# Expert blocks two batches earlier in the second layer, and the scatter ahead of them at twice the rate

## The chip, the cores and the metric

The kernel runs on one core of a Trainium2 chip. The metric is the device time of one execution in microseconds (us); the median of three runs before the change is 831.46 us (830.25 to 831.56). The engines are PE (TensorE, matrix products; PEld is its loading of weights), DVE (VectorE), ACT (ScalarE), POOL (GpSimd) and SP (SyncE, which issues most DMAs). Each works through its own queue of instructions in order and waits for the others on semaphores.

## The reference

The input x is 8 batches of 512 tokens with 128 features. Two layers follow one another, each of the form

```
xn = layernorm(x)
x  = x + attention(xn) * silu(ffn(xn))
```

Layer 0 has a causal attention with one head and a feed-forward part with a dense branch and 6 experts, of which two are taken per token. Layer 1, which the change touches, is

```
q = (xn @ Mq).reshape(B, 8, 512, 64)      # 8 heads of 64
k = (xn @ Mk).reshape(B, 8, 512, 64)
v = (xn @ Mv).reshape(B, 8, 512, 16)
s = softmax(q k^T / 8 over keys) v        # with the reference's own order of axes
e = argmax(xn @ Wg + bg)                  # one of 8 experts per token
y = relu(xn @ W1[e] + b1[e]) @ W2[e] + b2[e]
x = x + s * silu(y)
```

Everything is in float32.

## The kernel before

Layer 0 runs first, up to about 400 us of the span; the change does not touch it. It leaves the normalized rows of layer 1 in xn_all (32 tiles of 128 tokens, NT = 32), their transpose in xn2T, and a one-hot row of the chosen expert for each token.

Layer 1 has two kinds of work.

Attention goes batch by batch (B = 8), and within a batch over 16 steps, numbered through as k = 0 to 127 (IT = 16 in a batch). In step k PE makes two score tiles of 128 x 512 (score(k), L1334, called S(k) below) into a pair of PSUM banks; DVE takes their maximum (L1579); ACT takes the exp into pb and the row sums (L1446); DVE inverts the sums into rz (L1555); POOL scales the values by them into vs (L1255); and PE multiplies vs with pb (value(k), L1319, called V(k) below). PE runs value three steps behind score (LAG = 3): its queue holds S(k), V(k-3), then a "mixed" piece if the table MIXED has one for this step, then S(k+1). Mixed pieces are the projections of the next batch's q and k (L1293, one for every odd step), of its v (L1301, step 6), and the turning of finished heads (L1307, steps 4 and 12). DVE stores them (L1531, L1525, L1540) ahead of its rz of k-2 and its maximum of k. The first score of a batch waits until the last projection for it is stored. The bodies of the batches are written out, not looped.

The experts work on tokens sorted by expert. DVE computes from the one-hot rows a slot in DRAM for each token. Then POOL scatters the 32 tiles of xn_all to x_sorted by indirect DMA (L1243), one tile per DMA. SP waits until all 32 have landed (t_sc) and then loads blocks of 128 sorted tokens; there are NB = 39 blocks, each of one expert. A block is loaded, transposed by PE (L1374), multiplied with W1 (L1378), transposed again in four parts (L1386), multiplied with W2 (L1394), and stored to y_sorted by SP. The stages of following blocks overlap (function blocks). The 39 blocks run as one stretch on SP, PE, ACT and DVE, with no attention between them. Their buffers lie in xn_all, which the scatters have read by then.

Function layer1 sets the order for every engine: attention batches 0 to BEFORE-1, then all blocks, then attention batches BEFORE to 7. POOL has no blocks; it goes on with the next batch when rz arrives.

POOL's body counts a batch in 32 steps n (ST = 32, two for each k). At each n, in this order: scatters, if the batch lies before the blocks; at even n the vs of k = n/2; and, in batches 4 to 7 (kind SUMS), the gathers of y_sorted by indirect DMA (L1269, four in a row of n from 3 and from 19, each set for one quarter of the sum of two batches) and three products and sums over them (L1226, L1230, L1233). How many scatters have been issued after step `now` (counted through the batches from 0) is `(now + 1) * 3 // 8`, up to 32. In batches 4 to 7 ACT also takes a tanh of the gathered rows, and SP stores the output at the end of each sum.

Of the kernel before, what the change touches and what calls it, by code (L numbers as in the profile page):

```python
# [19 lines left out]
def recurrent_d2_kernel(nc, x, W, b, ln_g, ln_b, aw1, ab1, aw2, ab2, gate_w, gate_b, ew1, eb1, ew2, eb2,  # L20
# [9 lines left out]
    NT = B * TT  # L30
# [18 lines left out]
    with ExitStack() as ctx:  # L49
# [1114 lines left out]


        PLAIN, SUMS = range(2)
        BEFORE = 4
        GATHER_AT = (3, SH + 3)
        SUM_AT = (5, GEN + 5)
        LOAD = -2  # L1170
# [19 lines left out]
        def layer1(eng, body, make=None, enter=None, leave=None):  # L1190
            for bt in range(BEFORE):
                body(bt, PLAIN, False)
            if make:
                eng.wait_ge(t_ex, 1)
                if enter:
                    enter()
                blocks(eng, make)
                if leave:
                    leave()
            for bt in range(BEFORE, B):  # L1200
                body(bt, SUMS if bt >= B // 2 else PLAIN, bt == B - 1)

        @blk.gpsimd
        def _(pool):
# [16 lines left out]
            def sum_up(k, part):  # L1221
                rows = bass.ds(k * TT, TT)
                if part == 0:
                    pool.wait_ge(g_th, k * 2 + 2)
                    pool.wait_ge(g_st, k * 16 + 16)
                    pool.tensor_tensor(ob[:, :, :], th3[:, :, :], yg[:, :, :], ALU.mult).then_inc(g_c, 1)  # L1226
                elif part == 1:
                    pool.wait_ge(mb_free, turn_use(k * 2 + 1) + 1)
                    pool.wait_ge(g_c, k * 2 + 1)
                    pool.tensor_tensor(ob[:, :, :], ob[:, :, :], s1[:, rows, :], ALU.mult).then_inc(g_c, 1)  # L1230
                else:
                    pool.wait_ge(g_c, k * 2 + 2)
                    pool.tensor_tensor(ob[:, :, :], ob[:, :, :], x_all[:, rows, :], ALU.add).then_inc(g_o, 1)  # L1233

            def body(bt, kind, last):
                for n in range(ST):
                    if isinstance(bt, int) and bt < BEFORE:
                        if bt == 0 and n == 0:
                            pool.wait_ge(t_slot, 1)
                            pool.wait_ge(t_z, 1 + 16)  # L1240
                        now = bt * ST + n
                        for g in range(min(now * 3 // 8, NT), min((now + 1) * 3 // 8, NT)):
                            pool.indirect_dma_start(  # L1243
                                out=x_sorted, out_offset=bass.IndirectOffsetOnAxis(ap=slot[:, g:g + 1], axis=0),
                                in_=xn_all[:, g, :], in_offset=None).then_inc(t_sc, 16)
                    if kind == SUMS and n in (2, ST // 2 + 2):
                        pool.wait_ge(g_sl, (bt - 4) * 2 + n // (ST // 2) + 1)
                    if n % 2 == 0:
                        k = bt * IT + n // 2
                        s = k % SLOTS  # L1250
                        if n == 0:
                            pool.wait_ge(mb_free, values_in(bt))
                        pool.wait_ge(n_rz, k + 1)
                        pool.wait_ge(n_av, k + 1)
                        pool.tensor_tensor(vs[s][:, :, :],  # L1255
                                           vt[bt % 2][:, n // 2 % TT, :, :].rearrange("p j d -> p (j d)")
                                           .unsqueeze(1).broadcast_to([P, 2, D]),
                                           rz[:, 2 * s:2 * s + 2].unsqueeze(2).broadcast_to([P, 2, D]),
                                           ALU.mult).then_inc(n_vs, 1)
                    if kind == SUMS and n in (0, ST // 2):  # L1260
                        k = (bt - 4) * 2 + n // (ST // 2)
                        if n == 0:
                            for par in range(2):
                                pool.wait_ge(m_st[par], 16 * ((NB + 1 - par) // 2) + 16)
                        pool.wait_ge(g_o, k + 1)
                        pool.tensor_copy(slot_b[:, :], slot[:, bass.ds(k * TT, TT)]).then_inc(g_sl, 1)
                    t = n % SH - GATHER_AT[0]
                    if kind == SUMS and 0 <= t < TT:
                        pool.indirect_dma_start(  # L1269
                            out=yg[:, t, :], out_offset=None, in_=y_sorted,  # L1270
                            in_offset=bass.IndirectOffsetOnAxis(ap=slot_b[:, t:t + 1], axis=0)).then_inc(g_y, 16)

                    if kind == SUMS and 0 <= n % SH - 2 * SUM_AT[0] - 1 < 3 and not (last and n > SH):
                        sum_up((bt - 4) * 2 + n // SH, n % SH - 2 * SUM_AT[0] - 1)

            layer1(pool, body)
            for part in range(3):
                sum_up(B - 1, part)

        @blk.tensor  # L1280
        def _(pe):
# [117 lines left out]
            def enter():  # L1399
                pe.wait_ge(mb_free, pairs_in(BEFORE))  # L1400
                pe.wait_ge(n_e, 2 * BEFORE * IT + 4)

# [263 lines left out]
```

## Time and profile before

| what | value |
|---|---|
| median of the runs | 831.46 us (830.25 to 831.56) |
| profiled execution, its own time | 831.46 us |
| its span | 829.7 us |
| PE busy | 746.8 us (90%) |
| DVE busy | 582.6 us (70%) |
| ACT busy | 396.6 us (48%) |
| POOL busy | 238.7 us (29%) |
| mean granted clock of TensorE | 0.975 |

A profile is one execution. Spans are counted from its first instruction. "Busy" of an engine is the time in which it executes an instruction; the rest is waiting or issuing. Matmuls are pipelined and their ends are modelled. The granted clock is a share of full speed: 1.00 is 2.4 GHz, 0.50 is 1.2 GHz. In the timeline each row gives the start, the duration, the engine, the line, the operation, what it writes and reads, how many instructions are merged into the row, and in square brackets how long the engine was idle before it and what ended that. "issue" there means that it waited for nothing that the profile shows.

The stages of the span: layer 0 up to 399 us; sorting and the first projections to 417; attention batches 0 to 3 from 417.28 to 563; the blocks from 563.76 to 671.38; attention batches 4 to 7 with the sums from 671.38 to the end.

### The profile page before, as it was taken

The page shows a single profiled execution, that of the slowest core. Times are in us where ns is not written, and L with a number is a line of the kernel's source. Part 1 is how long each engine was busy: PE and PEld are TensorE (multiplying, and loading weights), DVE is VectorE, ACT ScalarE, POOL GpSimd, SP SyncE. Part 2 cuts the span into 40 slices and gives each one's busy share as a digit, 9 for nine tenths or more (in the row PEclk, how much of TensorE's full clock was granted, in tenths as well). Part 3 has the DMA queues.
Part 4 walks back from the last instruction along what each step waited for, and adds up shares of the span by engine and source line. Part 5 has one row for each costly group of instructions (what it writes and reads, how often), then busy time and mean ns, then how long its engine had stood idle before and what let it go on. Part 6 is the DMA issues. An engine that isn't in the chain of part 4 may idle for free. (4 is left out here: it accounts for less than half of the span.)

```text
span 829.7 us, 19914 instructions
## 1 busy us (share of the span) xinstructions
PE 746.8 (90%) x6611; PEld 497.9 (60%) x6612; DVE 582.6 (70%) x1486; ACT 396.6 (48%) x1000; POOL 238.7 (29%) x364
## 2 busy tenths in 40 slices
PE   5989899999999999992789999998999999999983
PEld 3666677888788788882334444444666754444331
DVE  5888864678778778786587878883333368778772
ACT  2332314444344344340056666664444557677782
POOL 7355200000000000000036565320000037676773
PEclk9999999999999999997799999999999999999996
DMA  8600000000000000000500000001111101111110
GB/s 262 209 0 0 1 1 1 1 2 0 0 0 0 0 0 0 0 0 0 150 14 25 23 23 23 11 3 29 51 47 50 48 25 30 30 27 27 40 33 19
DMA packets 34272, 25.04 MB, mean 30 GB/s; under 512 B 3303, under 2 KB 30626, under 8 KB 34210
## 3 DMA queue, kind: packets, MB, share of 16 engines
q1 hardware_dynamic: 31256, 19.48, 8.0%
q0 software_dynamic: 2048, 4.20, 1.8%
q8 instruction: 37, 0.61, 0.3%
q10 hardware_dynamic: 906, 0.55, 0.2%
q14 instruction: 25, 0.20, 0.1%
HBM read 14.91 MB, written 9.31 MB: 29 GB/s over the span
## 5 line engine op out<-in xcount | busy, mean ns | idle before, releaser
L1446 ACT ACTIVATE pb<-bank,nmx 128x512 f32<-128x512 f32 x256 | 173.2, 682 | 70.5 <-DVE nmx L1579 67.7
L1579 DVE TENSOR_REDUCE nmx<-bank 128x2 f32<-128x1024 f32 x128 | 156.4, 1223 | 30.7 <-PE bank L1334 29.2
L1334 PE MATMUL bank<-qk 64*128 64x512 f32 x512 | 144.2, 640 | 10.2 <-DVE qk L1531 5.3
L853 ACT ACTIVATE hid<-bank,cols 128x512 f32<-128x512 f32 x128 | 87.8, 687 | 123.6 <-PE bank L766 123.5
L1255 POOL TENSOR_TENSOR vs<-vt,rz 128x256 f32<-128x256 f32 x128 | 78.4, 613 | 231.0 <-DVE rz L1555 216.8
L1319 PEld LDWEIGHTS bank<-pb,vs 128*32 128x32 f32 x2048 | 48.6, 110 | 101.3 <-issue 72.0
L782 PEld LDWEIGHTS bank<-w_e,hid 128*128 128x128 f32 x768 | 98.1, 191 | 8.2 <-DVE acc L1000 1.7
L782 PE MATMUL bank<-w_e,hid 128*128 128x128 f32 x768 | 100.1, 275 | 0.0
L1319 PE MATMUL bank<-pb,vs 128*32 128x128 f32 x2048 | 83.3, 281 | 5.3 <-POOL vs L1255 5.3
L728 POOL TENSOR_TENSOR r<-ve,half_neg 128x4 f32<-128x4 f32 x8 | 8.1, 1011 | 274.0 <-DVE ve L927 274.0
L1462 ACT ACTIVATE xn_all<-bank,cols 128x128 f32<-128x128 f32 x156 | 44.5, 367 | 51.7 <-PE bank L1386 51.7
L1334 PEld LDWEIGHTS bank<-qk 64*128 64x128 f32 x512 | 38.8, 184 | 47.8 <-ACT pb L1446 25.4
L766 PE MATMUL bank<-xb_hi,w_u_hi 128*128 128x512 f32 x128 | 60.0, 469 | 3.3 <-DVE xb_lo L958 3.3
L1587 DVE COPY xn_all<-bank 128x512 f32<-128x512 f32 x39 | 27.0, 692 | 50.0 <-PE bank L1378 50.0
L1000 DVE SCALAR_TENSOR_TENSOR acc<-bank,wf,acc 128x128 f32<-128x128 f32 x160 | 44.9, 343 | 22.2 <-PE bank L782 20.9
L1531 DVE COPY qk<-bank 128x512 f32<-128x512 f32 x64 | 43.8, 689 | 13.5 <-PE bank L1293 12.5
L1446 ACT ACTIVATION_READ_ACCUMULATOR pb<-bank,nmx 128x1 f32 x256 | 50.5, 197 | 0.0
L766 PE MATMUL bank<-xb_hi,w_u_lo 128*128 128x512 f32 x128 | 50.4, 394 | 0.0
L766 PE MATMUL bank<-xb_lo,w_u_hi 128*128 128x512 f32 x128 | 50.3, 393 | 0.0
L1394 PEld LDWEIGHTS bank<-w,xn_all 128*128 128x128 f32 x312 | 37.9, 191 | 11.9 <-issue 11.7
L1293 PE MATMUL bank<-xn2T,mq 128*32 128x256 f32 x512 | 40.1, 385 | 3.6 <-DVE qk L1531 2.2
L1394 PE MATMUL bank<-w,xn_all 128*128 x312 | 41.6, 276 | 0.4 <-issue 0.4
(225 smaller groups left out, 1235.7 us busy)
## 6 DMA issues: line engine op xcount, KB each, us to landing
x_sorted<-zero SPq DMA_DIRECT2D x1, 2496.0 KB, 12.4
xn_all<-x_sorted SPq DMA_DIRECT2D x39, 64.0 KB, 1.8
y_sorted<-xn_all SPq DMA_DIRECT2D x39, 64.0 KB, 1.6
x_all<-in_L_attn_x_dram SPq DMA_DIRECT2D x8, 256.0 KB, 5.9
w<-in_L_ffn_W_dram SPq DMA_DIRECT2D x1, 2048.0 KB
out_dram<-xn_all SPq DMA_DIRECT2D x8, 256.0 KB
w_u<-in_L_ffn_ew_dram SPq DMA_DIRECT2D x1, 768.0 KB
w_e<-in_L_ffn_ew_dram SPq DMA_DIRECT2D x1, 768.0 KB
```

The source lines that it names most:

```text
L766: mm = pe.matmul(psum[n % NU][:, :], w[:, n * P:(n + 1) * P], x_[:, :], start=(i == 0), stop=(i == 2))
L782: mm = pe.matmul(dst[:, t * P:(t + 1) * P], hid[n % NU][:, t * P:(t + 1) * P], w, start=(first and t == 0), stop=last, skip_group_check=True)
L853: act.activation(hid[n % NU][:, :], psum[n % NU][:, :], ACT.Gelu, bias=col((ROW_AB1 if n < AC else ROW_EB1 - AC) + n), scale=1.0).then_inc ...
L1000: ins = dve.scalar_tensor_tensor(acc[:, t, :], y, wf[:, t, e:e + 1], acc[:, t, :], ALU.mult, ALU.add)
L1255: pool.tensor_tensor(vs[s][:, :, :], vt[bt % 2][:, n // 2 % TT, :, :].rearrange("p j d -> p (j d)") .unsqueeze(1).broadcast_to([P, 2, D]), ...
L1319: mm = pe.matmul(bank[c * 2 * VD:(c + 1) * 2 * VD, at:at + P], vs[k % SLOTS][:, ab, c * 2 * VD:(c + 1) * 2 * VD], pb[k % SLOTS * 2 + ab][: ...
L1334: mm = pe.matmul(psum[score_banks(k) + ab], qk[bt % 2][half, 1, h, 2 * m:2 * m + 2, :].rearrange("p a k -> p (a k)"), qk[bt % 2][half, 0, ...
L1394: mm = pe.matmul(psum[(5, 6)[par]][:, 0:D], hT[par][:, c * P:(c + 1) * P], w_2[:, bass.ds(e * HC + c, 1), :].rearrange("p a d -> p (a d)") ...
L1446: act.activation(pb[s + ab][:, :], psum[score_banks(k) + ab], ACT.Exp, bias=nmx[:, s + ab:s + ab + 1], scale=1.0, accum_out=zz[:, s + ab:s ...
L1462: ins = act.activation(hT[par][:, c * P:(c + 1) * P], psum[(2, 4)[par]][:, c * P:(c + 1) * P], ACT.Relu, bias=cols[:, bass.ds(e * HC + (RO ...
L1531: dve.tensor_copy(qk[bt % 2][:, :, :, g, :], mixed_bank(u)[:, :].rearrange("p (s h k) -> p s h k", s=2, h=HH)).then_inc(mb_free, 1)
L1579: dve.tensor_reduce(nmx[:, s:s + 2], banks[:, score_banks(k):score_banks(k) + 2, :], AX.X, ALU.max, negate=True).then_inc(n_mx, 1)
```

## The change

The number of attention batches ahead of the blocks goes from 4 to 2, and the scatters are issued at 3/4 per step n in place of 3/8, so that all 32 fall into the two batches.

```diff
         PLAIN, SUMS = range(2)
-        BEFORE = 4
+        BEFORE = 2
         GATHER_AT = (3, SH + 3)
...
                         now = bt * ST + n
-                        for g in range(min(now * 3 // 8, NT), min((now + 1) * 3 // 8, NT)):
+                        for g in range(min(now * 3 // 4, NT), min((now + 1) * 3 // 4, NT)):
                             pool.indirect_dma_start(
                                 out=x_sorted, out_offset=bass.IndirectOffsetOnAxis(ap=slot[:, g:g + 1], axis=0),
                                 in_=xn_all[:, g, :], in_offset=None).then_inc(t_sc, 16)
```

The sums stay in batches 4 to 7. Before, the scatters fell into steps 2 to 85 of 128; now into steps 1 to 42 of 64, at every n that is not a multiple of four.

## Rows read from the trace of the kernel before

**Rows 1.** The page, busy time: us, share of the span, instructions.
```profile
PE 746.8 (90%) x6611; PEld 497.9 (60%) x6612; DVE 582.6 (70%) x1486; ACT 396.6 (48%) x1000; POOL 238.7 (29%) x364
```
**Rows 2.** Windows, batches 1 to 3: stretch, length, busy per engine, clock, DMA, GB/s.
```profile
453.07:489.75 36.68, 35.58 (x464) 16.43 (x465) 30.02 (x52) 24.35 (x67) 21.86 (x28) 1.00 0.07 23
489.75:526.42 36.67, 35.58 (x464) 16.43 (x465) 30.02 (x52) 24.34 (x67) 19.84 (x26) 1.00 0.08 23
526.42:563.10 36.68, 35.58 (x464) 16.41 (x464) 30.05 (x51) 24.35 (x67) 9.80 (x16) 1.00 0.01 2
```
**Rows 3.** Timeline of PE, the first score of batch 1.
```profile
453.07 1.13 PE L1334 MATMUL bank<-qk 64*128 64x512 f32 x4 [0.91 <-DVE qk L1531]
```
**Rows 4.** Timeline of POOL: vs(0), first scatter, three rows around vs(3), vs(16).
```profile
423.14 0.61 POOL L1255 TENSOR_TENSOR vs<-vt,rz 128x256 f32<-128x256 f32 x1 [22.52 <-DVE rz L1555]
423.97 1.25 POOL L1243 DMA_INDIRECT x_sorted<-xn_all,slot  x1 [0.22 <-issue]
...
427.08 1.01 POOL L1243 DMA_INDIRECT x_sorted<-xn_all,slot  x1 [0.16 <-issue]
428.12 0.62 POOL L1255 TENSOR_TENSOR vs<-vt,rz 128x256 f32<-128x256 f32 x1
428.90 1.01 POOL L1243 DMA_INDIRECT x_sorted<-xn_all,slot  x1 [0.17 <-issue]
...
458.71 0.60 POOL L1255 TENSOR_TENSOR vs<-vt,rz 128x256 f32<-128x256 f32 x1 [1.31 <-DVE qk L1531]
```
**Rows 5.** Windows: the blocks, batches 4 and 5, the entry of the blocks.
```profile
563.76:671.38 107.62, 99.79 (x586) 70.87 (x586) 38.41 (x79) 51.30 (x195) 0.00 (x0) 0.98 0.16 46
671.38:708.05 36.67, 35.58 (x464) 16.41 (x465) 29.89 (x52) 24.53 (x65) 22.33 (x30) 1.00 0.10 26
708.05:745.19 37.14, 35.65 (x464) 16.42 (x465) 30.10 (x52) 26.57 (x71) 25.81 (x33) 1.00 0.11 30
...
565.00:570.00 5.00, 4.11 (x10) 1.75 (x10) 1.03 (x2) 1.54 (x6) 0.00 (x0) 0.68 0.09 28
```
**Rows 6.** Timelines of POOL, SP, PE: last scatter, first load, first product of the blocks.
```profile
518.35 1.01 POOL L1243 DMA_INDIRECT x_sorted<-xn_all,slot  x1 [0.15 <-issue]
...
521.51 0.81 SPq L1625 DMA_DIRECT2D xn_all<-x_sorted  x2
...
563.76 0.30 PE L1374 MATMUL bank<-ident,xn_all 128*128 128x128 f32 x1 [1.57 <-ACT pb L1446]
```
**Rows 7.** Timeline of PE, a value product of batch 5.
```profile
732.30 0.65 PE L1319 MATMUL bank<-pb,vs 128*32 128x128 f32 x16 [0.40 <-POOL vs L1255]
```
**Rows 8.** Timeline of POOL, two gathers in a row and the vs behind them.
```profile
681.86 1.00 POOL L1269 DMA_INDIRECT xn_all<-y_sorted,slot_b  x1
683.16 0.95 POOL L1269 DMA_INDIRECT xn_all<-y_sorted,slot_b  x1 [0.30 <-issue]
684.12 0.63 POOL L1255 TENSOR_TENSOR vs<-vt,rz 128x256 f32<-128x256 f32 x1
```
**Rows 9.** Timeline of PE: V(0), V(1), V(19), V(20).
```profile
423.81 0.64 PE L1319 MATMUL bank<-pb,vs 128*32 128x128 f32 x16
...
426.31 0.65 PE L1319 MATMUL bank<-pb,vs 128*32 128x128 f32 x16
...
467.11 0.64 PE L1319 MATMUL bank<-pb,vs 128*32 128x128 f32 x16
...
469.83 0.64 PE L1319 MATMUL bank<-pb,vs 128*32 128x128 f32 x16
```
**Rows 10.** Groups of POOL from 420 to 520 us: count, busy us, mean ns, idle before.
```profile
L1243 POOL DMA_INDIRECT x_sorted<-xn_all,slot x32 | 32.5, 1015 | 5.2 <-issue 5.2
```
**Rows 11.** Windows of 5 us, for the granted clock.
```profile
795.00:800.00 5.00, 3.80 (x46) 1.48 (x48) 3.55 (x5) 4.08 (x12) 3.00 (x5) 1.00 0.07 16
800.00:805.00 5.00, 3.73 (x56) 1.61 (x53) 3.27 (x7) 4.32 (x14) 4.69 (x7) 1.00 0.18 52
380.00:385.00 5.00, 0.00 (x0) 0.00 (x0) 4.39 (x9) 0.30 (x1) 0.00 (x0) 0.75 0.00 0
```

## The prediction

> **What bounds the kernel now.** I began with the busy times and the 40 slices, then cut the second layer into its stages with the windows view, and then read the timelines of POOL and PE side by side. The busy times give PE 90% of the span [rows 1], but the share is an average over two layers; what decides is the stage that the change touches. The windows by batch [rows 2] say more. In the second layer an attention batch takes 36.68 us with scatters on POOL (the batch at 453.07), 36.67 with scatters in about three quarters of it (at 489.75) and 36.68 with none (at 526.42). PE is busy 35.58 us in each. So PE paces these batches, and the scatters cost nothing today: taking them out of a batch gains nothing. The clock is 1.00 in all three, the 2.4 GHz level. PE's one long idle piece in a batch is the 0.91 us at its boundary [rows 3], where the first score waits for DVE to store a projection that PE itself has just made. It is a round trip behind PE's own work, so it moves with PE and absorbs no delay.
>
> The batch pace gives the budget. A batch is 16 steps k: per k a pair of scores S(k), then the value product V(k-3), sometimes a projection. 36.68 / 16 = 2.29 us for one k, 4.59 us for two. Per k POOL makes one vs of 0.61 us; an indirect DMA occupies it for 1.01 us [rows 4]. POOL's steps n are two to a k: n even holds a vs, and any n may hold a scatter, issued ahead of that n's vs.
>
> **The change, part by part.** It has two edits: BEFORE 4 to 2 moves the 39 expert blocks from behind batch 3 to behind batch 1, and the rate of the scatters goes from 3/8 to 3/4 per step n. Nothing is added or removed: the number of scatters (32), gathers, blocks and attention steps stays.
>
> *The move.* All queues carry the blocks together. Their 107.62 us [rows 5] stay, since their loads, products and stores are the same and POOL has nothing in them. At the entry PE waits for the last exp (1.57 us idle, [rows 6]) and a stretch of 5 us shows a mean clock of 0.68 [rows 5]; the batch ahead of the entry has the same order of work, so I leave both as they are. At the exit the next batch is now plain instead of one with gathers. The batch with gathers behind the blocks took 36.67 us [rows 5], as short as a plain one, so nothing is gained there. Of the later batches with gathers, the one at 708.05 took 37.14: 0.40 us of it is one value product that waited for vs [rows 7]. That hangs on when gathers land; I cost it at 0, with 0.5 us either way. On SP, the move brings the wait for all scatters nearer to the first load. Today the last scatter is issued at 518.35 and the first load starts at 521.51, 42 us ahead of the blocks at 563.76 [rows 6]. With the change the 32nd scatter falls in step n = 42, that is k = 21 of 32, and ten steps k, some 23 us, remain before the entry. The load, its landing and this wait stay hidden. If that cover were gone, each microsecond would be paid in full.
>
> *The rate.* Today's pattern has 3 scatters in 8 steps n (four k): POOL needs 4 x 0.61 + 3 x 1.01 plus gaps, under 6.5 us of 9.17. The new pattern has 3 scatters in 4 steps (two k): vs, scatter, scatter, vs, scatter. Starts in the timeline price it [rows 4, 8]:
> - vs to the DMA behind it: 0.78 us (428.12 to 428.90).
> - DMA to the vs behind it, POOL not waiting: 1.04 us (427.08 to 428.12).
> - DMA to DMA: the scatters of before never stand back to back; the gathers do: 681.86 to 683.16, 1.30 us, and 0.96 from the second to the vs behind it (683.16 to 684.12). For the second scatter of a pair I take 1.00 to its vs, the middle of 0.96 and 1.04.
>
> Two k then need 0.78 + 1.30 + 1.00 + 0.78 + 1.04 = 4.90 us of POOL against PE's 4.59. POOL becomes the bound for as long as scatters last. A late vs(k-3) holds V(k-3) at the head of PE's queue, and behind it the projection of this k and S(k+1), so DVE's maximum and ACT's exp of k+1 start late as well; both have slack (DVE is busy 30.02, ACT 24.35 us of a batch of 36.68), PE has none. What absorbs it first is the lead of vs over its value product. That lead is small at the start: vs(0) begins at 423.14 and V(0) at 423.81; V(1) starts at 426.31, so vs(1), which POOL then did right behind the first scatter, was in time; with two scatters ahead of it it is not [rows 4, 9]. At vs(19) the lead has been used up too. I walked POOL step by step from vs(0) to vs(21), letting each PE delay shift all later rz (rz comes from DVE, whose work follows PE's). Each rz is there before POOL reaches its vs (vs(16), which waited for DVE before, began at 458.71 [rows 4]; shifted by the 2.8 us that PE is late by then that is 461.5, and POOL gets there at 462.6), so POOL is never idle in the walk and the delay is plain POOL time.
>
> The last vs that PE must wait for is vs(19), in step n = 38. Before it POOL starts 19 earlier vs and 29 scatters (steps 1 to 38 less the nine multiples of four), 10 of them followed by another scatter, 10 being seconds of a pair, 9 single. So from the start of vs(0): 19 x 0.78 = 14.82; 10 x 1.30 = 13.00; 10 x 1.00 + 9 x 1.04 = 19.36; 0.24 more for the first scatter, which takes 1.25 instead of 1.01 [rows 4]; 0.61 for vs(19); and 0.06 to PE (vs ends at 423.75, V(0) starts at 423.81). Sum 48.09, and 423.14 + 48.09 = 471.23 us. Before, V(19) started at 467.11 [rows 9]. The delay is 4.12 us. vs(20) and vs(21) end ahead of their products as shifted (V(20) lies 2.72 us after V(19) [rows 9]; POOL gets from vs(19) to vs(20) in 0.78 + 1.04), so it grows no further. After that POOL has slack, but PE is the bound and full, so nothing is caught up: blocks and all later batches shift by 4.1 us.
>
> Bounds of the pair's cost: without any gap between two DMAs (1.04 and then 0.96) the sum is 10 x 0.30 less, a delay of 1.1 us; if every first DMA of a pair costs as the one at 423.97 (1.54), and the second 1.04, it is 2.8 more, 6.9 us. The value taken is that of the only back-to-back rows there are. A gain is excluded here: POOL is not the bound of any batch that loses its scatters.
>
> All 32 scatters of before but the first took 1.01 us on POOL (mean 1015 ns), with DVE busy 30.02 of 36.68 us [rows 2, 10]: nothing on DVE held them up. The Trainium skill, page "SBUF — State Buffer", section "SBUF: two separate sides", states the opposite case: a DVE operation in a two-port mode, an fp32 copy within SBUF above all, locks GpSimd out, and descriptors of a DMA issued there cannot be written meanwhile. By that rule the new price per scatter would rise with every such copy. The trace does not bear it out here; it is the third rival.
>
> The profiled execution took 831.46 us, of which 829.7 is span, and it equals the median of the three runs. So the forecast is 831.46 + 4.12 = 835.6 us.
>
> **The rivals.**
> 1. *The scatters stay hidden; not slower.* The place is POOL's queue between 423 and 476. It decides in the cost of two k on POOL: if that is under 4.59 us, the leads hold and nothing moves. For it: the lower bound comes to 0.78 + 1.04 + 0.96 + 0.78 + 1.04 = 4.60, just at the edge. Against: the gathers' 0.30 us gap between the two DMAs [rows 8]. Time 831.5. If, beside that, the clock did not dip at the entry, the 5 us at 0.68 there would shrink to 3.4 and give back 1.6 us: 829.9, and with the 0.4 of [rows 7] 829.5, just faster than the noise.
> 2. *The clock falls under the waits.* PE would wait about 0.2 us per k. The mean granted clock is 0.75 in the 5 us at 380 in which PE did nothing, and 0.68 at the entry, after the idle time there [rows 5, 11]. But from 795 to 805 PE was busy only 3.80 and 3.73 us of 5 and the clock stayed at 1.00 [rows 11]; here PE would be busy some 90% (35.58 of 36.68 + 2.8). Should it fall once, 5 us at the lower level (1.2 GHz) do the work of 2.5: 838.1, more if repeated.
> 3. *Scatters get dearer when denser*, by the 0.24 us that the first one shows: 29 x 0.24 = 7.0 more, 842.6. Against it are the 31 equal durations, and vs, which stayed at 0.60 to 0.63 us beside DVE. The lock that the Trainium skill's page "SBUF — State Buffer" states is a reason why it could be so.
> 4. *The entry waits for scatters or their landing.* 23 us of cover against 3.2 from the last issue to the load [rows 6]: a delay of more than 20 us of POOL would be needed. It would start at 836 and go up.
>
> **How the numbers follow.** Forecast (POOL bound, delay 2 to 6 us) 0.78; rival 1 0.14 (of which 0.04 is faster than noise); rival 2 0.03; rival 3 0.04; rival 4 0.01. Range: the bounds 832.6 (delay 1.1) to 838.4 (delay 6.9), with the 0.5 us of gather landings within; what lies outside is most of rival 1 and rival 3, under 2 in 10. A change within 0.2% (1.66 us) can't be told from none in this kernel: same is 829.8 to 833.1. That takes rival 1 without its faster part and a low end of the forecast, 0.14; faster 0.04; slower 0.82.
>
> **What would show it.** Right: in the changed profile 31 scatters still at about 1.01 us, pairs 1.30 apart; POOL without a wait for rz from 423 to 475; the value products of k = 1, 2, 3, 7, 8, 9, 11 and so on idle before them with POOL's vs as the releaser; the first batch some 2.8 us and the second 1.3 us longer than before; batches from the third on at 36.7 us; blocks at 107.6 us, starting near 494.5. Wrong: both batches at 36.7 (rival 1), a granted clock under 1.00 between 425 and 475 (rival 2), scatters of over 1.1 us (rival 3), or PE idle for a load at the first block (rival 4).

## The result, and the profile after

The changed kernel takes 838.95 us (median of 4 runs, 837.84 to 839.87); the kernel before, on the same chip, takes 831.48 us. The ratio is 1.0096, with a 95% interval of 1.0079 to 1.0114: 7.5 us slower. The forecast of 835.6 us had the sign and named the cause of most of it, but it is 3.4 us short, and 0.6 us outside its range. In two further comparisons, each on a chip of its own, the same kernel came out 1.0072 [1.0058, 1.0085] and 1.0063 [1.0048, 1.0077], 6.0 and 5.2 us slower.

The profiled execution of the changed kernel took 837.39 us (span 835.7), 5.9 us over the profiled one of before and less than any of the four timed runs, so some 1.5 us of the first comparison (838.95 against 837.39) lies in no trace. This execution itself lies inside the forecast's range; the median does not.

The page, busy time; it answers to [rows 1]. No engine does more work; the time is waiting and a lower clock.
```profile
PE 747.9 (89%) x6611; PEld 498.2 (60%) x6612; DVE 582.7 (70%) x1486; ACT 396.7 (47%) x1000; POOL 238.5 (29%) x364
```
Windows of the kernel after, with the columns of [rows 2]: batch 0, batch 1, the blocks, batch 2 (the first behind the blocks), and the batch that answers to the one of 37.14 us in [rows 5].
```profile
418.20:458.32 40.12, 34.06 (x413) 14.94 (x413) 29.47 (x51) 24.51 (x66) 29.41 (x35) 1.00 0.11 35
458.32:495.73 37.41, 37.16 (x464) 16.98 (x464) 29.22 (x50) 23.11 (x63) 21.11 (x28) 0.95 0.08 26
497.24:603.67 106.43, 98.39 (x586) 70.23 (x586) 38.42 (x79) 51.36 (x195) 0.00 (x0) 1.00 0.16 47
603.67:640.34 36.67, 35.58 (x465) 16.43 (x465) 30.12 (x53) 23.96 (x65) 9.80 (x16) 1.00 0.02 4
713.68:750.95 37.27, 35.72 (x464) 16.41 (x465) 30.12 (x52) 26.49 (x71) 25.73 (x33) 1.00 0.11 30
```
Batch 0 took 35.79 us before (first score at 417.28, first score of batch 1 at 453.07 [rows 3]); it takes 40.12 now, 4.33 more. The last batch ahead of the blocks, up to their first product, took 563.76 - 526.42 = 37.34 us [rows 2, 6]; it takes 497.24 - 458.32 = 38.92 now, 1.58 more, with a mean clock of 0.95 in the row that ends at 495.73. Behind the blocks a batch takes 36.67 us as before, and the blocks are 1.19 us shorter, since here the clock stayed at 1.00 through them (0.98 in [rows 5]). The first score came 0.92 us later, in code that the change does not touch. 4.33 + 1.58 - 1.19 + 0.92 is 5.64 of the 5.9 us; the rest is in the later batches (37.27 against 37.14 in the one above).

Timeline of POOL after, the same steps as in [rows 4]: each pair of scatters is as priced.
```profile
424.06 0.61 POOL L1255 TENSOR_TENSOR vs<-vt,rz 128x256 f32<-128x256 f32 x1 [22.36 <-DVE rz L1555]
424.89 1.25 POOL L1243 DMA_INDIRECT x_sorted<-xn_all,slot  x1 [0.22 <-issue]
...
428.21 1.01 POOL L1243 DMA_INDIRECT x_sorted<-xn_all,slot  x1 [0.17 <-issue]
429.25 0.62 POOL L1255 TENSOR_TENSOR vs<-vt,rz 128x256 f32<-128x256 f32 x1
430.04 1.01 POOL L1243 DMA_INDIRECT x_sorted<-xn_all,slot  x1 [0.17 <-issue]
431.35 0.96 POOL L1243 DMA_INDIRECT x_sorted<-xn_all,slot  x1 [0.30 <-issue]
432.33 0.62 POOL L1255 TENSOR_TENSOR vs<-vt,rz 128x256 f32<-128x256 f32 x1
```
430.04 to 431.35 is 1.31 us, 431.35 to the vs 0.98, and two k take 4.91 us (427.42 to 432.33). Over all 32 the scatter costs no more than before [rows 10], here the group of POOL from 420 to 480 us:
```profile
L1243 POOL DMA_INDIRECT x_sorted<-xn_all,slot x32 | 31.9, 998 | 6.9 <-issue 6.6 <-PE bank L1319 0.3
```
Timeline of PE after: two value products that wait for vs, then the boundary of batch 1, which answers to [rows 3], and what follows it.
```profile
428.10 0.65 PE L1319 MATMUL bank<-pb,vs 128*32 128x128 f32 x16 [0.80 <-POOL vs L1255]
...
433.01 0.64 PE L1319 MATMUL bank<-pb,vs 128*32 128x128 f32 x16 [0.52 <-POOL vs L1255]
...
458.32 1.13 PE L1334 MATMUL bank<-qk 64*128 64x512 f32 x4 [2.34 <-DVE qk L1531]
459.38 0.69 PE L1319 MATMUL bank<-pb,vs 128*32 128x128 f32 x16
459.99 2.08 PE L1334 MATMUL bank<-qk 64*128 64x512 f32 x4
462.00 1.08 PE L1319 MATMUL bank<-pb,vs 128*32 128x128 f32 x16
```
The boundary takes 2.34 us instead of 0.91, and the second score pair behind it 2.08 instead of 1.13. The windows show why: TensorE's clock is at its lower level, 1.2 GHz (0.50), from about 460 to 463.
```profile
460.00:462.00 2.00, 2.00 (x8) 0.50 (x4) 0.78 (x2) 1.26 (x4) 1.67 (x3) 0.50 0.10 33
462.00:464.00 2.00, 2.00 (x34) 1.23 (x32) 1.22 (x1) 0.82 (x4) 1.42 (x2) 0.69 0.10 33
```
So there are three things to explain: POOL's queue, which was forecast, and the longer boundary and the dip behind it, which were not.

### The profile page after: what moved, and what is told of

Its sections match the earlier page's. It is cut to its first block and busy times, and to the rows that moved or that the text cites. A ratio compares the mean times of both kernels' runs of the same rounds, so it can differ in the third digit from the quotient of the medians.

```text
span 835.7 us, 19914 instructions
## 1 busy us (share of the span) xinstructions
PE 747.9 (89%) x6611; PEld 498.2 (60%) x6612; DVE 582.7 (70%) x1486; ACT 396.7 (47%) x1000; POOL 238.5 (29%) x364
```

## The experiments

A common measure runs through them: the delay of a score against before, both counted from the kernel's own first score, so that layer 0 drops out. Before, S(15) starts 32.32 us behind the first score, S(16), the first of batch 1, 35.79, S(18) 39.92, and S(31), the last of batch 1, 69.00. I call what is added to the last one the loss of batches 0 and 1; the queue forecast is 4.12. Kernels in one group ran on one chip; "before" is the median there.

**First group (before 830.62 us): the change again, its half without the move, the move at a lower rate, and the scatters replaced by plain work.**

again, the change itself:

> The changed kernel itself, once more, for its profile. Theory A (POOL's queue alone): the loss is POOL's time per two k, the first batch has some 2.8 us of it, and every profile shows the same. Theory B (POOL's queue, and then PE's own stream): a projection's end is signalled about 1 to 1.5 us late once or twice while scatters are dense, and a dip of the clock follows; these differ from profile to profile, so the first score of batch 1 (0.91 us of idle before it in the kernel before, 2.34 in the changed one) may have another value this time. Time 838 to 840 by both.

836.6 us, ratio 1.0072 [1.0058, 1.0085]. In this profile (836.36 us) the boundary and what follows are as before, and S(31) is 4.22 us late. Timeline of PE, the boundary and a value product behind it:
```profile
456.20 1.13 PE L1334 MATMUL bank<-qk 64*128 64x512 f32 x4 [0.91 <-DVE qk L1531]
...
461.77 0.65 PE L1319 MATMUL bank<-pb,vs 128*32 128x128 f32 x16 [0.31 <-POOL vs L1255]
```
The kernel after and this one are the same program; their traces differ from the third projection on.

rate_only, shown against the kernel before:
```diff
-   range(min(now * 3 // 8, NT), min((now + 1) * 3 // 8, NT))    # BEFORE stays 4
+   range(min(now * 3 // 4, NT), min((now + 1) * 3 // 4, NT))
```


> BEFORE stays 4, only the rate of the scatters is 3/4. If the rate alone makes the loss: 836 to 839.5, with batches 0 and 1 as in the changed kernel and 2 and 3 at 36.7 us. If the move of the blocks has a part of its own: at least 2 us less than the changed kernel. If the clock's dip behind the scatters is what costs: the time differs from the changed kernel by one or two dips, 1 to 3 us, in either direction.

835.5 us, 1.0059 [1.0046, 1.0073], S(31) 4.22 us late: the rate alone costs what the queue forecast says, with the blocks where they were.

move_916: BEFORE = 2, rate 9/16.

> BEFORE is 2 as in the change, the rate of the scatters is 9/16: POOL then needs about 15.9 us for 16 steps n against PE's 18.3, and the last scatter is issued in step 56 of 64. Theory A and B: no wait for vs, 830.5 to 832.5, the move alone costs nothing. If the move has a cost of its own (entry, exit, late landing of the scatters): over 834.

832.99 us, 1.0024 [1.0015, 1.0033]. The loss of batches 0 and 1 is 0.14 us. What it costs lies at the entry of the blocks: the last scatter comes 14 steps n later, PE waits 1.90 us and for a load instead of 1.57 for exp, and the clock is at the lower level for some 6.8 us. Timeline of PE, the first product of the blocks:
```profile
491.92 0.30 PE L1374 MATMUL bank<-ident,xn_all 128*128 128x128 f32 x1 [1.90 <-DMA xn_all<-x_sorted]
```

busy: the change, with each scatter replaced by an addition on POOL of nearly the same duration. No scatter is issued, so the experts read zeros; SP waits for 32 counts of t_sc instead of 16 x 32, and an addition waits for the one two before it. The code is shortened at the dots.
```diff
-   pool.indirect_dma_start(out=x_sorted, ..., in_=xn_all[:, g, :]).then_inc(t_sc, 16)
+   row_x = x_all[:, 0:4, :]... [:, 0:496]
+   if g > 1: pool.wait_ge(t_sc, g - 1)
+   pool.tensor_tensor(scr[g % 2][:, :], row_x, row_x, ALU.add).then_inc(t_sc, 1)
```


> The changed kernel with each scatter replaced by an addition on POOL of about the same time in its queue (496 columns, some 1.25 us between the starts around it), so that x_sorted holds only zeros and no scatter DMA runs. Theory A: the time is POOL's, so the delay at the end of the scatters is as in the changed kernel, 836 to 839. Theory B: only the queue part of 2.8 to 4.1 us stays, no projection is signalled late and the clock does not dip behind batch 0: 834 to 836. If instead the traffic of the scatters makes all of it: 831 to 832.

828.88 us, 0.9977 [0.9968, 0.9986]: no loss (0.01 us by S(31)). I had missed the calibration: an addition takes 1.01 us like a scatter, but additions have no issue gap, so two k take 4.05 us. Timeline of POOL (line 1247 is the addition, 1257 the vs):
```profile
437.13 0.61 POOL L1257 TENSOR_TENSOR vs<-vt,rz 128x256 f32<-128x256 f32 x1 [0.34 <-DVE rz L1557]
...
441.18 0.61 POOL L1257 TENSOR_TENSOR vs<-vt,rz 128x256 f32<-128x256 f32 x1
```
It doesn't tell DMA from queue, but it shows that at 4.05 us for two k, under PE's 4.59, nothing is lost, and POOL waits for rz. That it is below before as a whole has its cause at the very end: POOL's closing DRAIN takes 4.01 us in busy and 6.6 us in every kernel with scatters. It is the last thing in the span, so times of kernels with and without scatters differ by 2.6 us for that alone, and the delays by S(31) are what can be compared.

**Second group (before 831.8 us): busy at the right size, and other rates.**

busy640: busy with 640 columns (x_all[:, 0:5, :]).

> The changed kernel with each scatter replaced by an addition of 640 columns on POOL, long enough that two k need about 0.57 + 1.25 + 1.25 + 0.57 + 1.25 = 4.9 us of POOL, as the scatters did (the 496 columns took only 4.05 us for two k, under PE's 4.59, and no value product waited). x_sorted holds zeros, no scatter DMA runs. Theory A (the loss is time in POOL's queue, whatever fills it): the value products wait for vs again, first score of batch 2 some 4.2 us late as with scatters, time about 4 us over that of the 496 columns. Theory B (it is the DMAs' traffic): about as the 496 columns, within 1 us.

832.07 us, 1.0002 [0.9993, 1.0011]. Timeline of POOL, two k:
```profile
437.24 0.61 POOL L1257 TENSOR_TENSOR vs<-vt,rz 128x256 f32<-128x256 f32 x1
437.81 2.46 POOL L1247 TENSOR_TENSOR scr<-x_all 128x640 f32<-128x640 f32 x2
440.23 0.61 POOL L1257 TENSOR_TENSOR vs<-vt,rz 128x256 f32<-128x256 f32 x1
440.80 1.25 POOL L1247 TENSOR_TENSOR scr<-x_all 128x640 f32<-128x640 f32 x1
442.01 0.61 POOL L1257 TENSOR_TENSOR vs<-vt,rz 128x256 f32<-128x256 f32 x1
```
Two k take 4.77 us. The prediction's sum with these starts is 19 x 0.57 + 10 x 2.42 + 9 x 1.21 + 0.61 + 0.06 = 46.59 us from vs(0) to V(19), against 43.97 before [rows 4, 9]: 2.62. The loss measured is 2.66. No scatter is on POOL here, so this loss is POOL's time and needs no transfers. As a whole the kernel equals before mainly because of the DRAIN, here in the views by line of before and of busy640:
```profile
L49 POOLq DRAIN  x1: 6625/6625/6625, 822.8 to 822.8; - x1
...
L49 POOLq DRAIN  x1: 4010/4010/4010, 826.1 to 826.1; - x1
```
Against busy, which has the same DRAIN but ran on another chip, it is 3.2 us slower.

move_58: BEFORE = 2, rate 5/8.

> BEFORE 2, scatters at 5/8 per step n: POOL needs about 17.2 us for 16 steps against PE's 18.3, and the last scatter goes out in step 51, some 13 us ahead of the blocks. Against 9/16 (2.4 us slower than before, last scatter in step 56, first block waits for its load) it tells whether the late landing is what the move alone costs: then 830.5 to 832. If the cost is the clock's dip at the entry of the blocks, which was 6.8 us long in the profiles with BEFORE 2 and 3.4 with BEFORE 4: again 832 to 833.5, with the long dip.

835.1 us, 1.0036 [1.0022, 1.005], loss 2.81 us by S(31), although POOL needs only 17.2 of 18.3 us in eight k. The need fits on average, but a pair of scatters falls on the start, where vs leads by least. Timeline of PE, V(2):
```profile
429.39 0.64 PE L1319 MATMUL bank<-pb,vs 128*32 128x128 f32 x16 [1.02 <-POOL vs L1255]
```

b3_half: BEFORE = 3, rate 1/2.

> BEFORE 3, scatters at 1/2 per step n (step 63 of 96 for the last): two k need 2 x (0.78 + 1.04) = 3.64 us of POOL. No wait for vs is expected. Within 0.7 us of the kernel before if the place of the blocks costs nothing; 1 to 2.5 us over it if moving them from behind batch 3 costs in itself.

832.03 us, 1.0000 [0.999, 1.0011], loss 0. The blocks can move by one batch for nothing when the rate keeps to single scatters.

before_again: the kernel before, as a candidate.

> The kernel before itself, for a profile from the same chip as these three. Same time within 0.2%. Its stages are what the others are compared with: batches of 36.67 us, blocks and entry 111.75 from the last score of batch 3 to the first of batch 4, of which the dip of the clock at the entry is a part that may differ from profile to profile.

832.21 us, 1.0001 [0.9991, 1.0011]: the comparison is good to 0.1%.

**Third group (before 831.47 us): the change twice more, and vs ahead of the scatters of a step.**

> The changed kernel a third time. POOL's queue alone: the first score of the blocks' entry some 4.2 us late against the kernel before (counted from the first score of batch 0). In the first profile of the changed kernel a projection was signalled 1.5 us late at the boundary of batches 0 and 1 and a dip of the clock followed (1.5 us more); the second profile had neither. If that is the common case on some chips, it stands here again and the time is 838 to 840; if it was rare, it is absent and the time is 836 to 838.

> One more profile of the changed kernel, for the same question: is a score of batch 1 late by more than POOL's queue explains, and how long is the clock's dip at the entry of the blocks (3.4 or 6.8 us).

again2: 836.71 us, 1.0063 [1.0048, 1.0077]; again3: 838.29 us, one run. Both profiles have the boundary of 2.31 us and the dip, S(31) 5.92 and 5.91 us late; again3 has a second dip at the entry of the blocks, at 499.1.

vs_first_34 and vs_first_58 (rates 3/4 and 5/8, BEFORE 2): the loop over scatters stands behind the vs of the step instead of ahead of it.
```diff
-   for g in range(...): pool.indirect_dma_start(...)      # scatters of step n
    if n % 2 == 0: ... vs of k = n/2 ...
+   for g in range(...): pool.indirect_dma_start(...)
```


> The changed kernel with the order in a step n turned round: vs first, then the scatter of the same n. The number of DMAs ahead of vs(19) falls by one, the rate stays. Rate theory (POOL needs 4.90 us for two k, PE 4.59): the loss is nearly the same, from the same sums 3.5 us instead of 4.1 at the end of the scatters. Burst theory (the scatter just ahead of a vs is what hurts, not the average): 2 us or less.

> The same turn at 5/8 per step, BEFORE 2. With the scatter first, 5/8 lost 2.8 us in batches 0 and 1 although POOL's average need (17.2 us for 16 steps) lies under PE's 18.3. Burst theory: with vs ahead the loss falls to 1.5 us or less, time 831.5 to 834. If the average were misjudged and POOL is the bound at 5/8 too, the loss stays at 2.5 us or more.

vs_first_34: 836.67 us, 1.0062 [1.0048, 1.0076], loss 5.25 us, more than the 4.22 of again and the 3.5 expected: my expectation was wrong. Behind a vs the order at 3/4 puts the pair ahead of an even k, and V(16) then waits 1.04 us for ACT's oT, which PE did not do before; the fourth group shows why. vs_first_58: 833.15 us, 1.0024 [1.0012, 1.0035], loss 1.78 against 2.81 in move_58, better, but above the 1.5 that I had allowed. Where the average fits, the order helps; at 3/4 it gained nothing.

**Fourth group (before 831.69 us): where the late boundary comes from.** Projections reach DVE late in some profiles. Timelines of DVE, its copies of the last three projections of batch 0, in the kernel after:
```profile
447.63 0.69 DVE L1531 COPY qk<-bank 128x512 f32<-128x512 f32 x1 [1.81 <-PE bank L1293]
452.56 0.69 DVE L1531 COPY qk<-bank 128x512 f32<-128x512 f32 x1 [0.50 <-PE bank L1293]
457.48 0.69 DVE L1531 COPY qk<-bank 128x512 f32<-128x512 f32 x1 [1.78 <-PE bank L1293]
```
and in again:
```profile
445.55 0.69 DVE L1531 COPY qk<-bank 128x512 f32<-128x512 f32 x1 [0.43 <-PE bank L1293]
450.89 0.68 DVE L1531 COPY qk<-bank 128x512 f32<-128x512 f32 x1
455.36 0.69 DVE L1531 COPY qk<-bank 128x512 f32<-128x512 f32 x1 [0.42 <-PE bank L1293]
```
In the first the copies stand 4.9 us apart, which is POOL's pace, and each begins at the end of POOL's vs (456.88 + 0.62 = 457.50, timeline of POOL after):
```profile
456.88 0.62 POOL L1255 TENSOR_TENSOR vs<-vt,rz 128x256 f32<-128x256 f32 x1
```
though the recorded end of the last projection is 1.5 us earlier (timeline of PE after):
```profile
455.36 0.61 PE L1293 MATMUL bank<-xn2T,mk 128*32 128x256 f32 x8
```
Four more profiles ask what decides it. shift2 and shift2b (the same kernel twice) let the scatters begin two steps later, which puts the pairs ahead of even k; projections come at odd k.
```diff
-   range(min(now * 3 // 4, NT), min((now + 1) * 3 // 4, NT))
+   range(max(0, min((now - 2) * 3 // 4, NT)), max(0, min((now - 1) * 3 // 4, NT)))
```


> The change (BEFORE 2, rate 3/4) with all scatters two steps n later: the step without a scatter is then n = 2, 6, 10 and so on, and the pair of scatters stands ahead of the vs of even k, not of odd k. Nothing else. The queue of POOL needs the same 4.90 us for two k, so by the queue alone it loses about 4 us in batches 0 and 1, give or take the 0.7 us of one vs: 835.5. The late projections of the changed kernel (DVE's copies of them at POOL's pace and 1.1 to 1.8 us of idle on DVE, and the first score of batch 1 after 2.3 instead of 0.91 us): if they come from how POOL's pairs lie to the projections of odd k, they are gone, PE waits 0.91 us at the boundary and the clock does not dip there: 835 to 836. If they come with the density of the scatters, whatever the place, they stay: 837.5.

> The same kernel as in the run before, a second profile: whether the boundary of batch 1 is the same (0.91 or 2.3 us) in both. If the place of the pairs decides it is the same; if the start decides by chance it may differ.

> BEFORE = 4 with the rate of 3/4, a second profile. Up to the end of batch 1 this kernel issues the same work as the changed kernel. If late projections come by chance in some executions, they may be seen here too, although the first profile had none; if they belong to the changed program (its code or its place in memory), the boundary is 0.91 us again and batches 0 and 1 lose 4.2 us.

> The changed kernel, a fifth profile. Three of four had the boundary of batch 1 at 2.3 us and a dip of the clock behind it, one had 0.91 us and no dip. By chance of the execution: either; by the chip: as the others of this chip.

shift2: 837.24 us, 1.0067 [1.0043, 1.0091]; shift2b: 836.01 us. From the second copy of batch 0 on, both have them at most 0.25 us behind the projection, and a boundary of 0.92 us, in shift2:
```profile
456.30 1.13 PE L1334 MATMUL bank<-qk 64*128 64x512 f32 x4 [0.92 <-DVE qk L1531]
```
But S(31) is 4.86 and 4.76 us late, as in vs_first_34 with a wait of 1.04 us for oT, so in time the shift is no better. Timelines of ACT and PE in shift2, ACT's copy of V(8) to V(15) out of PSUM and V(16), which waits for it:
```profile
463.49 0.60 ACT L1426 ACTIVATE oT<-bank 128x512 f32<-128x512 f32 x1 [1.67 <-PE bank L1319]
...
464.23 0.65 PE L1319 MATMUL bank<-pb,vs 128*32 128x128 f32 x16 [1.04 <-ACT oT L1426]
```
rate_only2, 838.34 us: the program that had no late projection in its first profile has them now, with the same 2.34 us and the clock at 0.50 from 458 to 461. Its timeline of PE and its window:
```profile
457.44 1.83 PE L1334 MATMUL bank<-qk 64*128 64x512 f32 x4 [2.34 <-DVE qk L1531]
```
```profile
458.00:461.00 3.00, 3.00 (x22) 1.10 (x20) 1.30 (x2) 0.44 (x1) 2.50 (x4) 0.50 0.13 44
```
again4, 837.03 us: late as well (2.29 us).

All profiles with the rate of 3/4 in one table, in us late against before, worked out from starts in the timelines of PE:

| profile | S(15) | S(16) | S(18) | S(31) |
|---|---|---|---|---|
| again, rate_only | 2.69 | 2.88 | 2.88 | 4.22 |
| after | 2.78 | 4.33 | 5.91 | 5.90 |
| again2, again3, again4, rate_only2 | 2.81 to 2.82 | 4.33 to 4.35 | 5.91 to 5.93 | 5.90 to 5.92 |
| shift2, shift2b | 2.75, 2.74 | 3.04, 3.03 | 3.04, 3.03 | 4.86, 4.76 |
| vs_first_34 | 3.45 | 3.74 | 3.74 | 5.25 |

So the same order of work has two courses, and 5 of 7 profiles took the one that is longer here. It is not the move (rate_only2 has it), and not the program (rate_only took both). What goes with it is the chip: the two short ones are the two profiles of one chip, the five long ones come from the others. On the chips of the third and fourth group all 4 profiles with the pair ahead of odd k are long, and all 3 with the pair ahead of even k (shift2, shift2b, vs_first_34) are not.

The traces also hold the time of every semaphore event, and these show where the delay sits. For the last projection of batch 0 in the kernel after, PE's event comes at 457.46, 1.48 us behind the recorded end of its last matmul, and DVE's copy starts 0.02 us behind the event. So DVE is not held up; PE's signal reaches it late. In again the event comes 0.04 us behind the end, though that end lies at the same place in a scatter (some 0.1 us behind its start in both). I counted the events of V(k) and of the q and k projections whose recorded end lies inside a scatter on POOL, and called an event late above 0.3 us:

| recorded end inside | the chip of again (3 profiles with scatters) | the other chips: the first comparison and the other three groups (13 profiles) |
|---|---|---|
| V(k), any scatter | 0 of 49 late | 167 of 180 late, up to 1.44 us |
| projection, the second scatter of a pair | 0 of 16 | 30 of 30, by 0.70 to 1.48 us |
| projection, any other scatter | 0 of 11 | 8 of 68 (2 not recorded) |

In busy and busy640, where additions stand in place of the scatters, none of 53 is late inside one. busy640 ran on one of these other chips: its gathers, which it keeps, have 11 of 15 V(k) late, and move_58 on the same chip has 14 of 15 inside scatters. So the delay needs the indirect DMAs on POOL, and it occurs in all profiles but those of one chip. The place of the pairs decides which signal it hits: ahead of odd k the projections (the long course), ahead of even k not the projections but V(15), whose event is 1.33 us late in shift2; that is the wait for oT. Even so it is not every signal of PE: the scores' events are mostly on time (1 of 10 late in the kernel after, 3 not recorded). Why these events come late beside the DMAs, and why not on one chip, no run shows.

## Why the prediction was wrong, point by point

**POOL's queue: right, mechanism and size.** Forecast 4.12 us; 4.22 us in the two profiles where nothing else comes in, 2.66 against 2.62 by the same sum in busy640, and 0.01 where two k need less than 4.59 us (busy). The pair was taken at 1.30 and 1.00 and is 1.31 and 0.98. Batch 0 was to lose 2.8 and loses 2.69 to 2.82 by S(15); batch 1 was to lose 1.3 and loses 1.34 in again. One detail is off: waits over 0.2 us stand only at odd k (1, 3, 9, 15, 17 in again), since V(2) started 0.06 us behind its vs without an idle time that shows.

**The step that failed is about [rows 3]: "It is a round trip behind PE's own work, so it moves with PE and absorbs no delay".** In 5 of 7 profiles it does not only move: PE's signal for the last projection, which fell into the second scatter of a pair, came to DVE 1.5 us late, and the idle time was 2.3 instead of 0.91 us. That is 1.5 us (4.33 - 2.82). The round trip hangs on what POOL issues, which the prediction left out. With the step went rival 2, held at 3 in 100. It did come, but not by the small waits that I priced it from: they left the clock at 1.00 in batch 0, in all profiles. Each of the five profiles with 2.3 us of idle PE at the boundary has the clock at 0.50 for some 3.4 us within 2 us behind it, and none of the others has, which adds 1.6 us (5.91 - 4.33); rival 2 had priced a fall at 2.5. Then batch 1 loses nothing more to POOL, where again loses 1.34: PE is so late that POOL has caught up, and POOL waits 1.50 us at 465.09. Timeline of POOL after:
```profile
465.09 0.60 POOL L1255 TENSOR_TENSOR vs<-vt,rz 128x256 f32<-128x256 f32 x1 [1.50 <-DVE qk L1531]
```
Together 4.22 + 1.5 + 1.6 - 1.3 = 6.0, and 5.9 is measured. I added POOL's loss to an unchanged rest; the rest depended on POOL too.

**The other half of that step, "I leave both as they are" of the blocks' entry and its dip: right on average, not in a single run.** From the last score ahead of the blocks to the first behind them it takes 111.75 us before (from S(63)). With a dip of 3.4 us as there, rate_only took 111.57, b3_half 111.94, again3 111.79; after, without a dip, 110.57; again, with 6.8 us of it, 112.69. So the place of the blocks costs nothing, and each 3.4 us at 1.2 GHz costs about 1.1 us there (rival 1 had hoped for 1.6 back). Three of the four profiles with BEFORE 2 that had a dip at the boundary had none at the entry (after, again2, again4), but shift2b had none at either, so the one need not follow from the other. From the first score to the first one behind the blocks the five profiles of the change are 4.6 to 6.0 us late (after 4.72, again 5.16, again2 4.64, again3 5.95, again4 4.57), against 4.12 forecast. That is why the median is much the same in both courses, and why the failed step cost 0.5 to 1.8 us of the miss and not all of it.

The blocks began at 497.24 instead of the forecast 494.5: 2.7 us later, of which 0.9 is layer 0 and 1.7 the boundary and the dip. The loads stayed hidden: the last scatter is issued at 476.97, 20 us ahead (timeline of POOL after).
```profile
476.97 0.96 POOL L1243 DMA_INDIRECT x_sorted<-xn_all,slot  x1 [0.30 <-issue]
```
Rival 4 is out for the change, but move_916 shows its edge: with the scatters ended 14 steps n later, 0.3 us of the load is uncovered.

**Rivals 1 and 3: wrong.** The scatters aren't hidden. They are not dearer when denser: 998 ns on average against 1015 [rows 10]. The Trainium skill's page "SBUF — State Buffer", section "SBUF: two separate sides", would have them wait for DVE's two-port copies. Nothing of that shows in the length of 32 scatters, but they hardly test it: every copy of DVE in this stretch is out of a PSUM bank, none within SBUF. A lock in the other direction, POOL's vs over DVE's copy, is out as the cause of the late copies: they start 0.02 us behind PE's event.

**What is still open.** Why PE's events come late beside indirect DMAs, and why never on the chip of again. And most of the miss in the first comparison: of the 3.4 us, 0.6 is the failed step with the entry in this profile (4.72 - 4.12), 0.9 is layer 0, which started the second layer between 417.05 and 418.48 us in all kernels, 0.3 the later batches (and the 0.1 by which the forecast rounds), and the other 1.6 is the distance of the median from the profiled execution, which no trace shows. The clock may be in it: its mean is 0.977 in the profiled execution and in the shortest timed one (837.84), and 0.971 in the other three (838.16 to 839.87). By my estimate 0.006 of 837 us is some 10 us more at 1.2 GHz, three pieces of 3.4 us; two of them at the blocks' entry, as again has them, would cost 2.2 us. Where they lay is not recorded. No version tried is faster than the kernel before with the whole work done; b3_half equals it.

## What to carry to other kernels

Price a queue's need over the shortest repeating group of steps, with gaps between instructions counted (1.01 us of scatter is 1.3 us next to another), against the pace of the engine that it feeds: 4.90 against 4.59 was the loss, with the size right to 0.1 us. A need that fits on average is not enough: at 5/8, with a pair at the start, 2.8 us were lost, at 9/16 0.1 (on the chip without late events). And where a loss is small beside the kernel, look at the waits that are already there and next to it: where a boundary grew from 0.9 to 2.3 us the clock fell behind it, and the two took 1.7 us more than the queue alone. To tell a late signal from a slow consumer, set the consumer's start against the semaphore event and not against the recorded end of the producer.

## What the runs showed of the hardware

- Two indirect DMAs in a row on POOL start 1.31 us apart, though each is busy for 1.0; two additions of 1.01 us start 0.97 apart. Equal busy time is not equal queue time.
- On all chips but one, PE's semaphore event came late, by up to 1.48 us, for work whose recorded end falls into an indirect DMA on POOL: 167 of 180 value products, and 30 of 30 projections in the second DMA of a pair. On the one chip it was 0 of 49 and 0 of 16, and with additions in place of the DMAs 0 of 53.
- So one program has two courses, told apart by the boundary (0.91 or 2.3 us) and 1.7 us apart at the end of batch 1 (4.22 and 5.91). The time as a whole does not tell them apart: 836.36 us in the profile of again (short), 836.71 in that of again2 (long).
- The clock at 0.50 came in pieces of 3.4 or 6.8 us, at the entry of the blocks in most profiles, and behind a boundary of batch 1 of 2.3 us in five of five, of 0.9 us in none.
- POOL's closing DRAIN took 6.6 us in the 16 profiles with scatters and 4.01 us in the two without, at the very end of the span.
